# Adding 126 unread TensorE products, in 32 places of the fill of a four-layer transformer kernel

## The reference, cut to what matters

```python
x = x + _L0_xattn_ref(_layernorm(x), ctx_1024, ctx_1024, mask, ...)
x = x + _L0_ffn_ref(_layernorm(x), Ws1, Ws2, W1, W2, Wr)
x = x + _L1_xattn_ref(_layernorm(x), ctx_1024, bias, wq, wk, wv, wo)
x = x + _L1_ffn_ref(_layernorm(x), q_w, k_w, v_w, o_w, sel_v_w, sel_o_w, route_scale)
```

## Time and profile before

| | us |
|---|---|
| median of 3 runs | 1430.54 |
| lowest, highest | 1429.03, 1432.64 |
| profiled execution, its own time | 1428.65 |
| its span | 1426.9 |
| TensorE busy | 1362.8 (96%) |
| VectorE busy | 1284.9 (90%) |
| ScalarE busy | 1219.8 (85%) |
| GpSimd busy | 921.2 (65%) |

### The profile page before, as it was taken

How to read it: one execution, slowest core, us unless ns; L and a number is a source line. 1 busy time by engine, 2 the same in 40 slices (tenths; PEclk the granted TensorE clock), 3 DMA queues, 4 the chain that set the end, 5 groups by cost and what they waited for, 6 DMA issues and landing times.

```text
span 1426.9 us, 34376 instructions
## 1 busy us (share of the span) xinstructions
PE 1362.8 (96%) x9585; PEld 923.6 (65%) x9585; DVE 1284.9 (90%) x5266; ACT 1219.8 (85%) x4234; POOL 921.2 (65%) x1409
## 2 busy tenths in 40 slices
PE   3578999999999999999999999999999999999997
PEld 2355666666666666666667666666666666666654
DVE  3768999999999999999999999999999999999986
ACT  3567888999888899988888998888899888889886
POOL 3123666676676667666666776667667666766777
PEclk7579999999999999999999999999999999999999
DMA  4530001000111100011110001111000111100000
GB/s 126 155 93 26 27 28 29 15 18 28 29 30 30 29 17 18 26 29 30 29 30 21 16 25 29 29 30 30 23 16 24 28 30 29 30 20 11 22 3 5
DMA packets 99967, 44.97 MB, mean 32 GB/s; under 512 B 21249, under 2 KB 99777, under 8 KB 99777
## 3 DMA queue, kind: packets, MB, share of 16 engines
q1 hardware_dynamic: 82560, 34.13, 8.6%
q10 hardware_dynamic: 17216, 8.65, 2.1%
HBM read 25.70 MB, written 8.52 MB: 24 GB/s over the span
## 4 chain that ended last, share of the span: by engine, by line
PE 87%; DVE 4%; POOL 3%; issue 2%; SPq 2%; ACT 1%; DMA 1%; POOLq 0%; ACTq 0%; DVEq 0%
PE psC L327 58%; PE psA L327 13%; PE psB L327 6%; PE psB L555 4%; PE psC L637 2%; SPq L3800 2%; DVE PTB L2366 1%; POOL accO L3413 1%; PE psA L489 1%; POOL TE L3401 1%; DVE nmA L2241 1%; DVE TE L2499 1%; POOL v_sb L3406 1%; PE psA L442 1%; PE psB L576 1%
## 5 line engine op out<-in xcount | busy, mean ns | idle before, releaser
L1341 ACT ACTIVATE TE<-psC,gateO 128x128 f32<-128x128 f32 x1024 | 290.0, 379 | 30.1 <-PE psC L327 27.0
L2499 DVE SCALAR_TENSOR_TENSOR TE<-psC,gateO,TE 128x128 f32<-128x128 f32 x1024 | 286.9, 342 | 21.7 <-PE psC L327 11.6
L1341 ACT ACTIVATE TE<-psC,gate 128x128 f32<-128x128 f32 x1024 | 299.2, 402 | 6.8 <-PE psC L327 1.9
L2499 DVE SCALAR_TENSOR_TENSOR TE<-psC,gate,TE 128x128 f32<-128x128 f32 x1024 | 284.1, 340 | 7.4 <-PE psC L327 3.0
L3413 POOL TENSOR_TENSOR accO<-accO,TE 128x512 f32<-128x512 f32 x192 | 247.0, 1286 | 53.9 <-DVE TE L2499 44.7
L327 PE MATMUL psC<-Oh,ch 128*128 128x512 f32 x512 | 269.0, 525 | 0.0
L327 PE MATMUL psC<-Vh,xTh 128*128 128x512 f32 x512 | 263.1, 514 | 0.7 <-ACT PS L1341 0.7
L3401 POOL TENSOR_TENSOR TE<-TE 128x256 f32<-128x256 f32 x256 | 189.8, 741 | 56.4 <-DVE TE L2499 41.4
L327 PE MATMUL psC<-Oh,cl 128*128 128x512 f32 x512 | 202.1, 395 | 0.0
L327 PE MATMUL psC<-Vh,xTl 128*128 128x512 f32 x512 | 201.6, 394 | 0.0
L327 PE MATMUL psC<-Vl,xTb 128*128 128x512 bf16 x512 | 199.7, 390 | 0.0
(11 more groups left out here) (231 smaller groups left out, 3391.0 us busy)
## 6 DMA issues: line engine op xcount, KB each, us to landing
bdB<-k_rows SPq DMA_DIRECT2D x128, 64.0 KB, 2.3
k_rows<-Kc SPq DMA_DIRECT2D x96, 64.0 KB, 2.0
Qs<-Qc SPq DMA_DIRECT2D x96, 64.0 KB, 1.9
raw<-in_L_ffn_v_w ACTq DMA_DIRECT2D x8, 512.0 KB, 4.0
raw<-in_L_ffn_o_w ACTq DMA_DIRECT2D x8, 512.0 KB, 3.9
x_sb<-in_x SPq DMA_DIRECT2D x32, 64.0 KB, 2.1
ctx_sb<-in_ctx SPq DMA_DIRECT2D x32, 64.0 KB, 2.0
Qb<-Qc SPq DMA_DIRECT2D x128, 8.0 KB
```

What stands on the lines that cost most here:

```text
L1341: return A.activation(o, i, func, **kw)
L2499: m = V.scalar_tensor_tensor(TE[:, i, e], psC[:, p, e * P:(e + 1) * P], gates[:, e:e + 1], TE[:, i, e], ALU.mult, ALU.add)
```

## The change

`warm` writes bank 3 of `psC` instead of bank 2, and calls of it stand in 32 places of TensorE's `start()`, 126 products in all. One product multiplies the bf16 identity (128x128, loaded as weights each time) by the same identity repeated four times: 512 columns. The only wait of `warm` is for the identity, which is there from the first microseconds on. All other lists are as they were.

```diff
             def warm(n):
                 pe.wait_ge(s_const, IDENT)
                 for _ in range(n):
-                    mm(heads_of(psC[:, 2]), ident_b[:], over_heads(ident_b[:], NJ))
+                    mm(heads_of(psC[:, 3]), ident_b[:], over_heads(ident_b[:], NJ))
```

More of the change, by code:

```diff
@@ L680, in start @@
                 a_ctxt(0)
+                warm(2)
                 a_keys(0)
+                warm(2)
                 a_values(0)
@@ L684, in start @@
                 a_xt(0)
+                warm(3)
                 a_queries(0)
+                warm(7)
                 products()
                 b_values(0)
+                warm(21)
                 a_scores(0, 0)
@@ L691, in start @@
                 a_scores(0, 3)
+                warm(5)
                 a_maxt(0)
+                warm(3)
                 a_scores2(0, 0)
@@ L696, in start @@
                 a_scores2(0, 3)
+                warm(5)
                 a_pvs(0)
+                warm(2)
                 a_ut(0)
+                warm(2)
                 a_att(0)
+                warm(2)
                 a_proj(0)
                 a_ctxt(1)
+                warm(2)
                 a_keys(1)
                 a_xt(1)
+                warm(4)
                 a_values(1)
+                warm(10)
                 a_x1t(0)
                 a_queries(1)
+                warm(2)
                 a_route(0)
                 a_shared(0)
+                warm(1)
                 a_ht(0)
+                warm(2)
                 a_ffn(0)
+                warm(9)
                 a_scores(1, 0)
```

## The result

| | before | after |
|---|---|---|
| median, 6 runs each (us) | 1429.01 | 1419.94 |
| lowest, highest | 1427.34, 1432.64 | 1418.40, 1420.25 |
| ratio of the medians | | 0.9929 (0.9915 to 0.9943) |
| span of the profiled execution | 1426.9 | 1418.3 |

The change makes the kernel 9.1 us faster by the medians and 8.6 us by the spans of the two profiled executions. I had forecast 1424.5 with a range of 1420 to 1431: the direction and the mechanism were right, the gain was half as large again as the 6.0 us of my sum, and the median lies a hair under the range.

The account below looks back on a forecast made before the run. TensorE bounds the kernel from 131 to 1420 us; the fill before it is a chain across engines at a partly halved clock. Terms sum to -6.0 us: 1428.65 to 1422.7, plus 1.9 for the median gives 1424.5, range 1420 to 1431.

Parts of the forecast that it names:

- The clock: TensorE in the fill: products filling its waits should hold 2.4 GHz, reading 1.00 from about 20 to 131 us.
- rival 1: Fill: clock not held everywhere, gains behind 54 us lost, 1429.8; a milder form loses 2 us; chance 0.14.
- The start: Up to the first scores: slow first products delay a_queries(0) and the DMAs of Qb and bdA, +0.4 us.
- Stage A of batch 0: 23.3 to 38.1 us: TensorE's pieces of the chain get shorter at the high clock, -2.1 us.
- To `a_scores(1, 0)`: 38.1 to 54.3 us: TensorE hardly on the chain, faster feed-forward of batch 0 hidden behind a DMA, 0.
- To the x of batch 1: 54.3 to 80.0 us: faster scores, transposes and products, partly covered by VectorE and ScalarE, -1.7 us.
- The feed-forward of batch 1 and behind: 80.0 to 91.1 us: limited by the Qb DMA, -0.4 us; then up to b_scores(1, 0), a further -0.8 us.
- The stretch at 102.4: 102.4 to 105.9 us: eight transposes and 32 products with V at the high clock, -1.4 us at x of batch 2.
- Behind the x of batch 2: After that x: clock already 1.00, SyncE's list sets the start of b_scores(2, 0) and moves as a whole, 0.
- rival 4: Fill: TensorE's whole chain share shrinks and hidden feed-forwards count, -9 to -10 us, 1420; chance 0.10.
- rival 2: Fill: ScalarE waits longer for weight slices (`raw`), taking half of 6.4 us of gains, 1427.3; chance 0.14.
- Rival 3: From 23.3 us on: clock stays at 1.2 GHz and products delay every step, +10 us, 1440; chance 0.07.

Follow-up runs that it names:

- e6: Changed kernel with half of each count of products, rounded down (57 in all): median 1424.78 us, ratio 0.9960.
- e8: Changed kernel with the same 126 products, each of 128 columns instead of 512: median 1425.34 us, ratio 0.9982.
- e3: Changed kernel without the first four calls (14 products), 112 products left: median 1424.76 us, ratio 0.9963.
- e11: Changed kernel without the 32 products in the three waits for DMAs ahead of a_scores of batches 0, 1, 2: median 1421.78 us, ratio 0.9949.
- e12: Changed kernel with 11 early products more, and 26, 17, 10 instead of 21, 9, 2 in the three DMA waits: median 1418.50 us, ratio 0.9930.
- e2: Changed kernel with only the first four calls (14 products), ahead of a_keys(0) to products(): median 1428.37 us, ratio 0.9990.
- e4: Kernel before, no products; ScalarE issues the first two expert slices only after the first scores: median 1428.84 us, ratio 0.9990.
- e13: Changed kernel, all 126 products; first two expert slices issued later, as relative to SyncE's DMAs before: median 1422.10 us, ratio 0.9942.
- e10: Kernel before, no products; eighth expert slice issued only after the first scores of batch 1: median 1432.38 us, ratio 1.0022.
- e14: Changed kernel, all 126 products; only the eighth expert slice issued later, as relative to SyncE's DMAs before: median 1422.66 us, ratio 0.9948.
- e7: Changed kernel with each count of products doubled (252): median 1429.80 us, ratio 0.9997.
- e9: Changed kernel with 11 products more, six ahead of selectors() and five ahead of a_ctxt(0): median 1419.42 us, ratio 0.9924.
- e15: Changed kernel, all 126 products; the first two and the eighth expert slices all issued later: median 1425.19 us, ratio 0.9964.
- e1: Changed kernel with only the first five calls (35 products): median 1426.86 us, ratio 0.9977.
- e5: Changed kernel, all 126 products; ScalarE issues the first two expert slices only after the first scores: median 1419.98 us, ratio 0.9931.

## Why the prediction was right or wrong

**What bounds the kernel: right.** What the fill had gained at `b_scores(2, 0)` (127.55 before, 119.23 after, 8.3 us) arrived at the end (8.6 us).

**The clock: right, and the base of the gain.** It was 1.00 from 23.3 on, the 32 products with V of batch 0 took the 1.1 us foreseen, and e6 and e8, which lose the clock, lose somewhat under half and some three quarters of the gain. The large wait before `a_scores(1, 0)`, from which my first rival started, was there (2.1 us empty behind nine products), and the profiled clock held all the same. The rival is real in weaker fillings: e3, e6 and e11. In its mild form it may be present in the change too, and there the profiled run was lucky: the mean clock of the six runs is 0.999 in three, the profiled one among them, and 0.996, 0.997 and 0.998 in the others, where e12, with its loss of 4 us, shows 0.998. Their times (1419.81 to 1420.25) lie within 2 us of the rest (1418.40 to 1420.08). The stretches with transposes, which the prediction named beside rival 1, did not fall back: eight transposes take 1.04 us at 65.13 and at 96.27 in the changed kernel, against 1.92 in the same places before.

**The start: the step that failed.** "+0.4 us" was exact for SyncE's issues (12.79 to 13.20) and wrong for the first scores. I wrote that the first expert loads "may start up to 1 us earlier or later; ScalarE is idle then", and looked only at who waits for a slice. The slices are under way while the small DMA that the scores wait for lands, and its landing depends on how far ahead of it they were issued. Term mis-sized: +0.4 foreseen, -0.7 measured (23.34 to about 22.6), which e2, e4 and e13 put on the landing (1.1 us shorter). The sign of the term was wrong for this one omission.

**Stage A of batch 0: right.** -2.1 foreseen including the first scores; -1.7 measured behind them, where I had -1.8. The two weight cuts passed the shift on as said.

**To `a_scores(1, 0)`: "0" was the second failure, of the same kind.** SyncE's issues moved by 2.66 us, as much as the x of batch 0. But the scores moved by about 3.7. The faster feed-forward, which I called hidden, let ScalarE (whose copy `hs` waits for its products) issue the seventh and eighth slices 4.2 us earlier (47.22 to 43.00 and 49.95 to 45.72), out of the way of the last four `bdA` issues. The DMA share before, in the two microseconds in which the scores waited, was

```profile
52.00:53.00 1.00, 0.00 (x0) 0.00 (x0) 0.93 (x6) 0.13 (x1) 0.00 (x0) 0.50 1.11 331
53.00:54.00 1.00, 0.00 (x0) 0.00 (x0) 1.00 (x2) 0.00 (x0) 0.94 (x2) 0.50 0.64 178
```

a full set of DMA engines and an idle TensorE. e10 confirms that this slice sets the landing; e14 shows the landing late again in the changed kernel (3.3 us for 2.5), with ScalarE held up beside it. 0 foreseen, -1.0 measured.

**To the x of batch 1: mechanism right, size slightly high.** -1.7 foreseen from the first scores of batch 1 on, some -1.2 measured: most of TensorE's time there was indeed covered by VectorE and ScalarE.

**The feed-forward of batch 1 and behind: right.** `a_scores(2, 0)` now waits for a DMA and no longer for x:

```profile
83.26 0.29 DVE L2362 TENSOR_TENSOR x<-psA,x 128x128 f32<-128x128 f32 x1 [0.86 <-PE psA L327]
...
85.99 0.24 PE L327 MATMUL psA<-late_b,ident_b 128*128 128x176 bf16 x1 [2.33 <-DMA Qb<-Qc]
```

The feed-forward ended 2.4 us sooner relative to the x of batch 1 and the step behind it moved by 0.4 or so; -0.4 and -0.8 foreseen, -1.5 measured. The stretch at 102.4 gave -1.6 (foreseen -1.4).

**Behind the x of batch 2:** 0 foreseen, -0.6 measured: 0.4 up to `b_scores(2, 0)`, where the wait for `Qs` is shorter, and 0.3 behind. I have no experiment on it.

**The rivals.** The size of rival 4 came out, but not by its cause: TensorE's own time in the feed-forwards stayed hidden, and the DMA landings made most of the difference. My sign for rival 2, ScalarE waiting longer for `raw`, did appear. Up to 131 us, in the kernel before and then in the changed one:

```profile
ACT Vh L1341 <- DMA raw<-in_L_ffn_v_w: 5.3, 4, 2.5
ACT Oh L1341 <- DMA raw<-in_L_ffn_o_w: 2.3, 2, 1.5
```

```profile
ACT Vh L1373 <- DMA raw<-in_L_ffn_v_w: 7.8, 5, 2.7
ACT Oh L1373 <- DMA raw<-in_L_ffn_o_w: 6.4, 4, 2.7
```

That is 14.2 us instead of 7.6, and the gain came all the same, so the sign was no proof of the rival's loss. Whether some of these waits stand on the chain and cost a part of a larger gain was not tested. Rival 3 did not happen. e7 shows what standing on the chain costs even at the high clock, about 10 us: the 42 products ahead of the first scores last 9.2 us in place of a 5.7 us wait, and the first maxima come 6 us later than in the changed kernel.

**The forecast as a number.** I added 1.9 us to go from the profiled execution to the median of three runs. That median, 1430.54, was itself high: over six runs it is 1429.01, and on the chips of the experiments 1428.61 to 1430.45. So of the 4.6 us between forecast and result, 1.5 are the base, 2.6 the sum against the shift of the profiles (-6.0 and -8.6), and 0.5 that the medians moved more than the profiles did. The lower range bound, 1420, rested on a rival that counted only chains of instructions and no DMA. With the two landing terms (-1.1 and -1.0) the sum would have been -8.1.

## What to carry to other kernels

Filling TensorE's waits with unread products is worth it where the clock falls in a latency-bound stretch, and the count matters in both directions: half left half of the gain, double took all of it. Size each filling to its wait at the high clock. Some ahead of the first waits brought the clock up earlier here (e9); a gain in time from it isn't shown. When a step gets faster, follow every DMA that it releases and ask which small, awaited DMA is in flight then; a large load that nobody waits for yet can be the most expensive neighbour. A late DMA can be followed by a second loss, through the clock behind the wait (e13).

## What was not expected of the hardware

- The DMA of keyrow (4 KB) landed the later the closer two 512 KB slices were issued ahead of it. With the first of them 1.1 to 1.8 us ahead it took 4.4 to 4.9 us (kernel before, e3, e6, e8, e10, e13, e15), with 2.1 to 2.7 us 3.5 to 4.0 (e7, e9, e12), with 2.8 to 3.5 us 3.1 to 3.3 (changed kernel, e1, e2, e11, e14), and with no slice under way 1.7 us (e4, e5).
- Early work brought the clock up early: with six products from 2.19 us on (e9), those at 5.51 us start 0.24 us apart, and the ctx transpose at 8.08 us took 0.33 us instead of 0.48.
- The length of one empty piece did not tell whether the clock would fall. The three of 2.1 to 2.3 us behind the products in the three DMA waits did not cost the changed kernel's profiled execution its clock, and one of 3.27 us in e13 did; but in e6 the first scores still took 0.38 us behind an empty 3.51 us (the clock fell after 24 us), and the kernel before lost it at 102.4 us after 3.4 us in which TensorE was busy for 1.97 and never idle for more than 0.8 at a time.

```profile
99.00:102.40 3.40, 1.97 (x14) 1.01 (x14) 3.40 (x27) 3.39 (x11) 0.99 (x1) 1.00 0.00 0
```
